# Unit products on TensorE ahead of the first conditioning products and in its early waits, in an attention and recurrent block

## The reference

```python
x = x + attention(condition(x, id1))      # part 1
x = x + ffn(adapt(x, id2))                # part 2
# condition: y[b] = x[b] @ W[id1[b]].T + bias[id1[b]], one of 8 matrices for each sequence
# attention (16 heads of 16): sim = q @ k.T / 4 / temp
#   scores = sum over 5 frequencies of alpha[h, f] * sin(2 pi sim / freq[f] + phi[h, f])
#   w = sigmoid(scores); w = w / (sum(w) + 1e-10); out = (w @ v) @ Wo.T + bo; layer norm
# adapt: x + relu(x @ W1[id2] + b1) @ W2[id2] + b2, layer norm, with the language's gamma and beta
# ffn: a gated recurrence over the 32 sequences, each step with the state of the one before:
#   c = sigmoid(.) * c + sigmoid(.) * tanh(.), then h = tanh(x @ wo.T + c @ uo.T + bo)
```

## Time and profile before

| what | value |
|---|---|
| median of three runs | 321.89 us (321.49 to 322.88) |
| the profiled execution's own time | 323.39 us |
| its span, first to last instruction | 321.6 us |
| busy: TensorE, VectorE, ScalarE | 89%, 85%, 80% of the span |
| instructions | 7374, of them 2686 matmul records |
| moved by DMA | 31.97 MB, mean 99 GB/s |
| chain that ended last, by engine | VectorE 39%, TensorE 32%, ScalarE 14%, issue 8%, DMA 3% |
| mean granted TensorE clock | 0.983 of full |

### The profile page before, as it was taken

The page is one execution under the profiler, slowest core; times in us unless marked ns, Lnnn a source line. Parts: engine busy times, 40 slices in busy tenths (PEclk is TensorE's granted clock), DMA queues, the critical chain, the costliest instruction groups (busy, mean ns, idle before and its releaser), DMA issues.

```text
span 321.6 us, 7374 instructions
## 1 busy us (share of the span) xinstructions
PE 285.4 (89%) x2686; PEld 177.5 (55%) x2686; DVE 274.6 (85%) x598; ACT 257.3 (80%) x378; POOL 51.6 (16%) x58
## 2 busy tenths in 40 slices
PE   0787898969889989999999998899999999998971
PEld 0576647866546855554575645556665545543350
DVE  3049996999999999999999998999999998554265
ACT  1069998999999999999999999899999894422132
POOL 5000600041100012332100214140013331210000
PEclk9999997998999999999999999999999999999997
DMA  5698427544044248045445240330444160020007
GB/s 174 244 388 303 93 30 227 116 135 67 0 91 117 30 113 242 0 75 118 103 88 143 74 68 1 71 70 15 108 106 67 35 150 16 2 34 2 0 0 261
DMA packets 32374, 31.97 MB, mean 99 GB/s; under 512 B 10706, under 2 KB 24274, under 8 KB 32338
## 3 DMA queue, kind: packets, MB, share of 16 engines
q1 hardware_dynamic: 27410, 26.67, 29.1%
q0 software_dynamic: 4352, 4.20, 8.7%
q10 hardware_dynamic: 576, 0.64, 0.8%
HBM read 23.36 MB, written 2.10 MB: 79 GB/s over the span
## 4 chain that ended last, share of the span: by engine, by line
DVE 39%; PE 32%; ACT 14%; issue 8%; DMA 3%; POOL 2%; SPq 1%; DVEq 0%; ACTq 0%; POOLq 0%
DVE sc L1626 12%; PE pg L694 7%; DVE ang L1615 5%; PE pg L685 5%; DVE ang L1606 5%; ACT ang L1130 4%; PE pf L491 3%; PE pav L589 3%; ACT ang L1139 3%; PE pf L571 2%; PE pf L547 2%; DVE fc L1761 2%; ACT sc L1121 2%; DMA w<-x 1%; DVE vz L1596 1%
## 5 line engine op out<-in xcount | busy, mean ns | idle before, releaser
L1139 ACT ACTIVATE ang<-ang,qs 128x2560 f32<-128x2560 int32 x32 | 77.4, 2433 | 0.3 <-DVE ang L1615 0.2
L1626 DVE SCALAR_TENSOR_TENSOR sc<-ang,ratio,sc 128x512 f32<-128x512 f32 (+1 forms) x120 | 73.0, 637 | 0.4
L1130 ACT ACTIVATE ang<-sc,phase 128x512 int32<-128x512 f32 (+1 forms) x110 | 64.5, 650 | 0.0
L685 PE MATMUL pg<-gate_w,zT 128*64 128x384 f32 x256 | 50.8, 499 | 0.6 <-DVE zT L1751 0.4
L694 PE MATMUL pg<-gate_u,cT 128*64 128x384 f32 x256 | 47.7, 493 | 1.6 <-DVE cT L1770 1.5
L1615 DVE TENSOR_SCALAR ang<-ang 128x2560 int32<-128x2560 int32 x32 | 47.5, 1501 | 0.0
L1606 DVE TENSOR_SCALAR ang<-sc,phase 128x256 int32<-128x256 f32 (+1 forms) x90 | 32.4, 412 | 2.6 <-ACT sc L1121 2.5
L1179 ACT ACTIVATE gat<-pg 128x384 f32<-128x384 f32 x32 | 15.6, 487 | 22.7 <-PE pg L694 22.3
L694 PEld LDWEIGHTS pg<-gate_u,cT 128*64 128x64 f32 x256 | 16.4, 136 | 22.1 <-issue 15.0
L513 PE MATMUL pf<-wc,xg 128*64 128x256 f32 x128 | 17.1, 416 | 9.5 <-DMA wc<-in_cond 8.8
L1149 ACT ACTIVATE sc<-sc,lead 128x512 f32<-128x512 f32 (+1 forms) x40 | 23.4, 628 | 2.3 <-DVE sc L1626 2.2
(11 more groups left out here) (114 smaller groups left out, 474.1 us busy)
## 6 DMA issues: line engine op xcount, KB each, us to landing
wc<-in_cond SPq DMA_DIRECT2D x30, 257.0 KB, 3.5
w<-in_up SPq DMA_DIRECT2D x32, 128.5 KB, 2.6
wa<-in_down SPq DMA_DIRECT2D x32, 66.0 KB, 1.9
xt<-in_xt SPq DMA_DIRECT2D x8, 256.0 KB, 3.0
xt<-rows POOLq DMA_DIRECT2D x8, 256.0 KB, 4.2
w<-x POOLq DMA_DIRECT2D x8, 256.0 KB, 4.2
xg<-in_x SPq DMA_DIRECT2D x3, 512.0 KB, 5.1
qm<-qT SPq DMA_DIRECT2D x48, 32.0 KB, 2.1
```

Source lines behind the costliest of these rows:

```text
L685: pe.matmul(pg[n % 2][u * L:(u + 1) * L, 0:GCOLS], zT[:, q % 2, kc, t * L:(t + 1) * L], gate_w[:, kc, u, :], start=False, stop=(kc == KC - ...
L1130: op = act.activation(ang[:, n % SLOTS, f, r], unit(n)[:, r], ACT.Identity, scale=TURN / FREQS[f], bias=phase[:, p * NF + f:p * NF + f + 1])
L1139: act.activation(a.bitcast(F32), a, ACT.Sin, scale=2 * PI_LOW / TURN, bias=qs[:, 3:4]).then_inc(sine_ready, 1)
L1626: op = dve.scalar_tensor_tensor(out=unit(n)[:, r], in0=ang[:, n % SLOTS, f, r].bitcast(F32), scalar=ratio[:, p * NF + f:p * NF + f + 1], i ...
```

## The change

The change puts 22 unit products ahead of the first conditioning product and 2 ahead of `turn_tokens(0)`. It raises the number in the waits before `scores(0)`, `queries(0, 1)` and `scores(1)` from 3 to 4, before `values(0, 0)` from 4 to 9, before `condition(1, 0)` from 4 to 9, and before `scores(2)` from 7 to 9. It lowers the number before `queries(1, 0)` from 5 to 3 and takes away the 2 before `scores(4)`. Everything else on TensorE, and everything on the other engines, stays in its order.

```diff
--- before.py
+++ after.py
@@ -730,35 +730,37 @@
 
             pe.wait_ge(eye_s, 16)
             pe.wait_ge(eye_s, 16)
+            warm(22)
             condition(0, 0)
             condition(0, 1)
+            warm(2)
             turn_tokens(0)
             warm(2)
             queries(0, 0)
             keys(0, 0)
-            warm(3)
+            warm(4)
             scores(0)
-            warm(3)
+            warm(4)
             queries(0, 1)
             keys(0, 1)
-            warm(3)
+            warm(4)
             scores(1)
-            warm(4)
+            warm(9)
             values(0, 0)
             values(0, 1)
-            warm(4)
+            warm(9)
             condition(1, 0)
             condition(1, 1)
             condition(2, 0)
             condition(2, 1)
             warm(3)
             turn_tokens(1)
-            warm(5)
+            warm(3)
             queries(1, 0)
             keys(1, 0)
             queries(1, 1)
             keys(1, 1)
-            warm(7)
+            warm(9)
             scores(2)
             weighted(0)
             weighted(1)
@@ -775,7 +777,6 @@
             output_bias(0)
             output_projection(0, 0)
             output_projection(0, 1)
-            warm(2)
             scores(4)
             warm(9)
             turn_residual(0)
```

## The result

The median of 20 runs is 320.73 us, against 322.68 us for 20 runs of the kernel before. The ratio is 0.9946, with a 95% interval of 0.9923 to 0.9968: 1.7 us faster, between 1.0 and 2.5. One of the 20 runs of the change took 1575.56 us; the ratio leaves it out, the median does not. The other 19 lie between 319.94 and 321.95 us, a spread of 2.0; those of the kernel before lie between 320.50 and 324.77, a spread of 4.3. The profiled execution took 320.29 us, 3.1 less than the profiled one of before (323.39).

The account below looks back on a forecast made before the run. No engine alone bounds it; the chain of waits does, with a serial TensorE start at half clock. From the median 321.89, -1.5 (start, limited by a transfer) and -0.4 (clock near 50 us) give 320.0 us; range 318.4 to 322.3.

Parts of the forecast that it names:

- The 22 products: Kernel start: clock rises 4.0 us into them, conditioning takes half as long, queries and keys end 2.7 us earlier.
- The products in the waits: Ahead of values and second group's conditioning: delays up to 0.5 and 0.4 us, 0.9 together; the other added ones free.
- What is late next: Second group's conditioning: third pair waits for a matrix landing at 31.7, so the gain there is 1.5 us, not 2.7.
- The clock near 50 us: Ahead of `scores(2)`: two more products keep the clock up, 0.8 us in the profiled execution, 0.4 for the median.
- From 60 us to the end: After 60 us, VectorE and ScalarE carry the gain on; it passes undiminished to the end.
- The slower case: Start: unit products do not raise the clock, conditioning stays at half speed, everything is later, about 325.0 us; chance 0.08.
- The whole gain: Rival: more of the start's 2.7 us comes through, with all 0.8 at 50 us, giving 318.9 us; chance 0.10.
- fall elsewhere: Before `turn_residual(0)`: idle 2.9 us, clock low for a second stretch, costs 1.5, giving 321.5; chance 0.24, including gain eaten.
- fall across the turning: Between conditioning and queries the clock falls again, the 2.7 shrinks to 1.0, giving 321.4 us; chance 0.08.

Follow-up runs that it names:

- 22 alone: Kernel before with only the 22 unit products ahead of the first conditioning; ratio to before 0.9934, median 320.35 us.
- 4 for 9: The change with 4 instead of 9 products ahead of `values(0, 0)` and of `condition(1, 0)`; ratio to the kernel before 0.9923.
- the five wide products: Kernel before with 5 unit products of 512 columns ahead of the first conditioning, in place of the 22 of 128; ratio to before 0.9941.
- the 19, the load order and the 9: Kernel before with 19 first products, second group's conditioning matrices loaded in order of use, 9 products ahead of `scores(2)`; ratio 0.9919, median 319.61 us.
- 44: Kernel before with only 44 unit products ahead of the first conditioning; ratio to before 1.0110, median 325.36 us.
- two at 50 us: Kernel before with 9 instead of 7 products ahead of `scores(2)`, nothing else; ratio to before 0.9985.
- eight fewer: Kernel before without the 3 and the 5 products around `turn_tokens(1)`; one execution, 320.40 us beside 321.81 for the kernel before.
- the 14: Kernel before with only 14 unit products ahead of the first conditioning; ratio to before 0.9936.

## Why the prediction was right

**The result.** Forecast was 320.0 against 321.89, a ratio of 0.9941; measured was 0.9946. The median of the kernel before turned out at 322.68 with more runs, and the change's, 320.73, lies inside the stated range. That the two ratios agree so closely is partly luck. For an execution like the profiled one I had forecast 321.1 us, 2.3 less than before, and the profiled one took 320.29, 3.1 less: the start came nearly as I said, what limits the stretch behind it was not what I said, the shorter spreading I did not have at all, and near the end 0.6 us were lost.

**The 22 products.** Forecast: they end at 9.4, conditioning ends at 11.3, the keys end at 14.6. Measured: conditioning from 9.6 to 11.6, and the first qT, right behind the keys, at 15.04 instead of 17.34: 2.3 us, not 2.7. More than half of the 0.4 is a later start: `eye` is there at 2.85, not at 2.6. The products themselves took 6.81 us, and I had 6.8, with the clock rising after 3.4 us where I took 4.0. The rest lies in small errors of the handoffs.

**The products in the waits.** Forecast up to 0.9 on the second group's conditioning; it is 2.30 - 1.46 = 0.8 (31.21 to 29.75). This was right.

**What is late next.** This step was wrong in its mechanism and right in its size. I let the last matrix land at 31.7 and hold up the third pair, and then the turned tokens decide at 35.95. The last matrix is issued at 26.10 in the profile after, and lands 4.7 us later, at 30.8:

```profile
wc<-in_cond SPq DMA_DIRECT2D x1, 257.0 KB, 4.7
```

The third pair wants it at 31.6 (29.75 + 1.84), so TensorE does not wait for it. What failed here is the 5.5 us from issue to landing, which I carried over from one profile. TensorE does not wait for any other matrix either, since the unit products hold it until the first pair's has landed; turning ends at 35.71 and VectorE comes to `yT` at 35.88 from its own list. What limits it is the five products ahead of the values: VectorE waits 0.5 us more there. The runs with 22 alone and with 4 for 9 do wait for a matrix, but for the first pair's; only with the five wide products is there a wait of 0.25 us at the third pair too. The term was -1.5 and measured -1.7 (41.76 to 40.04): its size is right by luck.

**The clock near 50 us.** Forecast 0.8 in an execution like the profiled one, 0.4 in the median. The fall costs 1.1 to 1.3 where it happens. The two more products are not what keeps the clock in the change: with 22 alone and 7 products it stayed as well, with 1.03 us of idle time, which had become shorter by a cause that I did not see, the next one. Nor does the length of the idle time alone decide, as I had let it: behind the same 2.45 us near 65 the clock fell in six profiles and stayed in six. For the median, the timed runs help. A stretch of 3.41 us at half speed takes 0.005 off a run's mean granted clock. Of 78 executions of the kernel before, 22 have a mean of 0.984 or less, as the profiled one has (0.983), which is two such stretches ahead of the one at the very end, near 50 and near 70 in that profile; 7 have 0.993 or more, and so none. Of the 19 of the change none is under 0.987, and 14 have one stretch (0.990 or less). If the fall near 50 is independent of the others, it comes in 22/78 divided by 14/19, or about 0.4 of the executions. That is an estimate, and with it the term is 0.4 times 1.1 to 1.3, some 0.5 us. I had 0.4.

**What I did not have.** The spreading is 1.0 us shorter (6.25 to 5.28), and no instruction transfer falls into it any more. From `yT` to `scores(2)` it is 11.97 us before and 11.00 after. This is a large term of the profiled difference, and no work was changed there. What sets the place of the transfer is not shown, nor how often it lies there in executions that were not profiled.

**From 60 us to the end.** I let the gain pass undiminished. Up to 275 us it nearly does: VectorE's second division is 3.78 us earlier and its last residual 3.68 (278.83 to 275.15). Then, in the profile after, GpSimd's last addition by DMA takes 5.32 us in the chain; from that residual to VectorE's next addition it is 6.59 us, 5.70 before, and 0.6 us are lost at the end. Over all profiled executions the time from the division to the end varies from 265.5 to 267.2 us, with the kernels' code behind 60 us the same but for unit products in one or two waits. A part of this is the clock again, near 304 us, under the last products of the second part (line 719). With the 19, the load order and the 9, the longest of all with 267.2:

```profile
303.58 1.99 PE pg L719 x8
```

The same products take 1.12 us in the profiles of before and after, and 1.33 to 1.59 in four others. From 304 to 306 us the granted clock of that kernel is 0.50, so a fall adds 0.9 us to its profiled span, in code that its edit does not touch.

**The sum.** In the profiles: -1.7 at the start, -1.0 by the spreading, -1.1 by the clock near 50, +0.6 by the late addition, and some 0.1 at the second fall: -3.1. In the timed runs it is -1.7. The profiled execution of the kernel before had the fall and the late rise at 17.1, the worst of both, and the long issue too. In the profiles of kernels without first products the first qT stands between 15.65 and 17.34, at 16.4 in the mean of five; with them, 44 aside, between 14.36 and 15.56, at 14.9 in the mean of seven. By these profiles, one of each kernel, the start gives 1.5 us on average and not 2.3, of which 0.6 are handed back at the values. It is a rough estimate: two of the five also have two products ahead of the turning, and whether these bring the rise forward was not tried. How much of the 1.0 of the spreading reaches the timed runs is open as well.

**The rivals.** The slower case did not come: unit products raise the clock, with no other work beside them. Its sum was also wrong: 321.89 + 3.2 + 0.9 is 326.0, not 325.5. The whole gain (318.9) did not come either. The clock did not fall elsewhere for longer: near 68 it stays low for one stretch, as before. The idle time there is 2.45 us and not the 2.9 that I had, since with the 2 products gone `scores(4)` waits 0.51 us for VectorE. No fall across the turning is seen in any run; with the change the first queries take 1.13 us. At `yT` the 22 alone give 2.4 us, and with the products of the waits 1.7. The rule of the Trainium skill (TensorE: Matmul & The Clock Gate, Part 1) that the ramp costs less than 1% of a span holds: the start gave 0.5% to 0.7%. The sentence of the Trainium skill in the same place, that the number of slow products differs between executions of one kernel, is what the first products show: the 22 took 6.68 to 7.44 us in four profiles. I should have carried it into the term.

## What to carry to other kernels

Where a kernel begins with a wait for data and then a serial stretch on TensorE, unit products that end just as the data lands give back the halved clock of that stretch. Many more delay all of it by their full length: with 22 more, `yT` came 4.6 us later than with the 22, and the kernel was 3.5 us slower than without any. Between 14 and 22 the timed runs show no difference. In a wait further on, count the products against the idle time that the row shows: two waits with 0.57 and 0.67 us were each filled with 1.1 us more, and handed back 0.6. Before a single profile is taken for the kernel, look at other executions too: here the profiled one of before held a fall of the clock and a long issue, worth 2 us, and by the granted clocks the fall does not come in every execution. The same holds for an experiment: that the clock stays in one profile shows nothing of the products put there, if it stays in other kernels' profiles without them.

## What the runs showed of the hardware

The moment at which TensorE's clock rises differs between executions of the same code. With the conditioning starting between 8.5 and 8.9 us, the queries behind it still ran at half speed in two profiles (2.02 and 1.86 us for the first four records and the handoff to the keys) and at full speed in three (1.13 us). Three of the five, before, two at 50 us and eight fewer, have the same list on TensorE up to there, and have the first qT at 17.34, 17.16 and 15.65. Under unit products alone, the rise came 3.4 us after the first of them in the profile after, and not within 5.6 us with the 14.

Where an instruction transfer on q8 fell into the run of small issues on SyncE, one issue took 0.91 to 1.65 us instead of 0.60, in four profiles of four; in the nine without it none was long. In the profile before, with 8 such issues in the path, this made the spreading 1.0 us longer.

GpSimd's inverse root of a variance (lines 406 and 409, two instructions on 2 columns) varies. The 22 alone, then the five wide products, at the same place in the program:

```profile
208.11 0.21 POOL L406 TENSOR_SCALAR rs<-mv 128x2 f32<-128x2 f32 x1 [2.11 <-DVE mv L1724]
208.41 1.88 POOL L409 TENSOR_TENSOR rs<-rs,mhalf 128x2 f32<-128x2 f32 x1
```

```profile
209.05 2.21 POOL L406 TENSOR_SCALAR rs<-mv 128x2 f32<-128x2 f32 x1 [2.23 <-DVE mv L1725]
211.34 0.72 POOL L409 TENSOR_TENSOR rs<-rs,mhalf 128x2 f32<-128x2 f32 x1
```

The first instruction took 0.21 and 2.21 us, the second 1.88 and 0.72, and VectorE's norm behind them came 3.40 us after its aggregate (line 1725) and not 2.55, 0.85 more, in the second kernel. What holds GpSimd there was not tried. This, the late addition and the clock near 304 us each account for 0.6 to 0.9 us of what differs from execution to execution behind 60 us.
